# A decoder layer on one core: the second causal mask moves from GpSimd to TensorE

## The chip, the core and the metric

The kernel runs on one core of a Trainium2 chip. A core has five engines that run side by side and meet through semaphores: TensorE (PE, matrix products, with weight loads of its own shown as PEld), VectorE (DVE), ScalarE (ACT), GpSimd (POOL) and SyncE (SP, which issues transfers). Products land in PSUM, eight banks of 128 partitions by 2 KB; all else lies in SBUF. The metric is the time of one execution in microseconds (us).

## The reference, cut to what matters

Sixteen sequences of 128 tokens by 128 features go through one layer: a minimal GRU (three gates and a scan), causal self-attention with 16 heads of 8 features, a gated feed-forward block, cross-attention to a context, and a mixture of eight experts of which two are chosen. The part that the change touches is the softmax of the self-attention:

```python
mask = (kidx <= W + j) & (kidx >= j + 1) & ((kidx >= W) | (cidx > 0))
scores = jnp.where(mask[None, None], scores, jnp.finfo(scores.dtype).min)
attn = jax.nn.softmax(scores, axis=-1)
out = jnp.einsum('bhcqk,bhckd->bhcqd', attn, vv)
```

A sequence is one window of 128, so this is plain causal attention: query q sees keys up to q.

## The kernel before

**Tiles.** Each of the 16 sequences is one tile k of 128 by 128. Every stage is a small function of k, and every engine has a list, written out by hand or by a planner, that says in which order it runs these functions for all tiles: PE 542 entries, ACT 485, DVE 510, POOL 226, SP 74. An engine runs its list strictly in order; an entry waits on semaphores (`after`) for its inputs. Tiles are pipelined: while the last stages of one tile run, the first stages of tiles far ahead are under way. Most buffers have two copies (`b = k % 2`).

**PSUM banks.** `HOME` gives each stage and tile one of the eight banks. `bank_free` makes PE wait until the last user of that bank has been read.

**Start.** SP and ACT issue the loads. PE runs 9 warming products (`keep_busy`, 128 by 512, on data that nobody reads), turns the weights (`w_gru`, `w_qkv`, `w_gate`, `w_ei`, ...) as their transfers land, and starts the GRU of the first tiles (`gru_turn`, `gru_gates`, `gru_turn_back`) and the projections of the context (`ctx_turn`, `ctx_project`). ACT evicts nearly all of that.

**Attention.** Queries and keys are split into three bf16 parts, go through DRAM (`parts_save`, `parts_stack` on SP) and come back stacked over 72 partitions so that one bf16 product has fp32 accuracy. `scores(k, n)` computes four heads with queries on partitions into a bank (four products of L897); one more product, the identity times the constant `above` (L899, 296 columns: only those behind MROWS = 53), adds -1e30 above the diagonal. DVE takes the row maxima (`maxima`), POOL splits them (`max_split`), PE turns them (`max_turn`), ACT copies them, SP puts them into the stacked queries (`max_stack`). `scores_turned(k, n)` then computes the same four heads with keys on partitions, maximum already subtracted (four products of L919, each a group of its own). ACT takes the exponential of the bank (`exponentials`, L1705). That result is not masked yet: two times a tile POOL's `keep_causal` (L523) zeroes the entries of later keys in two of the four banks at once, columns from 53 on. `att_values` waits for both selects (`att_kept`) and multiplies by the values, 32 column-tiled products.

**The rest of a tile.** `att_back`, `att_turn`, `att_project`, the feed-forward block (`ffn_*`, L964 and L987), cross-attention (`xat_*`), experts (`moe_*`, L1046). POOL computes the powers of -0.5 for all norms (`*_power`, L464), residuals, and part of the experts' sum. The last tile ends on DVE with `moe_layernorm(15)`; SP stores the rows.

Of the kernel before, what the change touches and what calls it, by code (L numbers as in the profile page):

```python
# [5 lines left out]
P = 128  # L6
# [8 lines left out]
MROWS = SROWS - QROWS  # L15
# [15 lines left out]
    "w_gru": "0",  # L31
    "gru_turn": "6130635251015364",
    "gru_gates": "6564665631347415",
    "w_qkv": "1",
    "ctx_turn": "0751373176661643",
    "w_ox": "4",
    "gru_turn_back": "7115525220167562",
    "w_gate": "3",
    "qkv_turn": "2043375324264473",
    "w_kq": "4",  # L40
    "qk_project": "2102272754237473",
    "w_ei": "0",
    "w_ej": "2",
    "v_project": "1610750457135003",
    "ctx_project": "7051505346162653",
    "w_m0": "0",
    "w_up": "2",
    "scores": "3127056563626562452440236442443333403164421350137725676407743707",
    "w_out": "4",
    "max_turn": "0245200515644061",  # L50
    "w_m1": "7",
    "probs": "0403141313405274312373664520265241600260432415523754465205655757",
    "att_values": "4410675465665645",
    "att_back": "3474671451562134",
    "att_turn": "5602511353530173",
    "att_project": "5175052773534032",
    "ffn_turn": "2015063551744601",
    "ffn_gate": "5367621631374704",
    "ffn_up": "3115173226106260",
    "ffn_down": "3671500753312560",  # L60
    "xat_turn": "1410670705106321",
    "xat_scores": "4737600607156332",
    "xat_turn_probs": "6712150724311715",
    "xat_values": "3333726551352157",
    "moe_turn": "1726034121131434",
    "moe_logits": "6007031017147427",
    "moe_experts_0": "0774730225456601",
    "moe_experts_1": "4226576422270232",
}
WEIGHTS = ("w_gru", "w_qkv", "w_ox", "w_gate", "w_kq", "w_ei", "w_ej", "w_m0", "w_up", "w_out", "w_m1")  # L70
READER = {
    "w_gru": "w_gru",
    "gru_turn": "gru_xT",
    "gru_gates": "gru_tanh",
    "w_qkv": "w_qkv",
    "ctx_turn": "ctx_T",
    "w_ox": "w_ox",
    "gru_turn_back": "gru_x1",
    "w_gate": "w_gate",
    "qkv_turn": "qkv_xT",  # L80
    "w_kq": "w_kq",
    "qk_project": "qkv_rest",
    "w_ei": "w_ei",
    "w_ej": "w_ej",
    "v_project": "max_v",
    "ctx_project": "ctx_kv",
    "w_m0": "w_m0",
    "w_up": "w_up",
    "scores": "max_max",
    "w_out": "w_out",  # L90
    "max_turn": "max_mT",
    "w_m1": "w_m1",
# [28 lines left out]
att_scores_ps att_p att_kept att_vT_ps att_vT att_o_ps att_rd att_o att_oT_ps att_oT att_y_ps att_x2  # L121
# [12 lines left out]
def decoder_layer(nc, x, ctx, mask, w_mix, Wg, bg, Wv, bv, Wd, bd, w_attn, Wqkv, Wo, w_ffn, Wgate, Wup,  # L134
# [4 lines left out]
    with ExitStack() as stack:  # L139
# [23 lines left out]
        above = sb("above", [P, 4, P], BF16)  # L163
        rows_q = sb("rows_q", [P, P], BF16)
# [108 lines left out]
        def _(sp):  # L273
# [93 lines left out]
            parts_save(3)  # L367
            load_ctx(3)
            max_stack(1)
# [14 lines left out]
            parts_stack(7)  # L384
            parts_save(8)
            max_stack(6)
# [3 lines left out]
            max_stack(8)  # L390
            store(0)
            parts_stack(9)
            parts_save(10)
            max_stack(9)
            parts_stack(10)
            store(1)
            store(2)
# [3 lines left out]
            store(3)  # L401
            max_stack(10)
            parts_stack(12)
            parts_save(13)
            parts_stack(13)
            max_stack(11)
            parts_save(14)
            parts_save(15)
            max_stack(12)
            parts_stack(14)  # L410
            max_stack(13)
            parts_stack(15)
            store(4)
            max_stack(14)
            max_stack(15)
            store(5)
# [13 lines left out]
        def _(pool):  # L430
# [35 lines left out]
            def gru_power(k):  # L466
                b = k % 2
                power(ss[:, 0, b:b + 1], rs[:, 0, b:b + 1], "gru_ss", k, "gru_rs", "gru_xn")

            def qkv_power(k):  # L470
                b = k % 2
                power(ss[:, 1, b:b + 1], rs[:, 1, b:b + 1], "qkv_ss", k, "qkv_rs", "qkv_xn")

            def ffn_power(k):
                b = k % 2
                power(ss[:, 2, b:b + 1], rs[:, 2, b:b + 1], "ffn_ss", k, "ffn_rs", "ffn_xn")

            def ffn_ln_power(k):
                b = k % 2
                power(mv[:, 0, b, 1:2], lrs[:, 0, b:b + 1], "ffn_mv", k, "ffn_rs1", "ffn_y1")  # L480

            def xat_ln_power(k):
                b = k % 2
                power(mv[:, 1, b, 1:2], lrs[:, 1, b:b + 1], "xat_mv", k, "xat_rs", "xat_y2")

            def moe_ln_power(k):
                b = k % 2
                power(mv[:, 2, b, 1:2], lrs[:, 2, b:b + 1], "moe_mv", k, "moe_rs", "moe_out")
# [52 lines left out]
            gru_power(0)  # L541
            gru_power(1)
            gru_power(2)
            gru_decay(0)
            gru_power(3)
            gru_power(4)
            gru_decay(1)
            qkv_power(0)
            causal_tiles()
            gru_decay(2)  # L550
            qkv_power(1)
            qk_low(0)
            gru_power(5)
            gru_decay(3)
            qkv_power(2)
            gru_power(6)
            gru_decay(4)
            qk_low(1)
            qkv_power(3)
            gru_decay(5)  # L560
            qkv_power(4)
            gru_power(7)
            gru_decay(6)
            qk_low(2)
            max_split(0)
            qkv_power(5)
            gru_power(8)
            qk_low(3)
            qkv_power(6)
            keep_causal(0, 0)  # L570
            max_split(1)
            keep_causal(0, 1)
            qk_low(4)
            max_split(2)
            keep_causal(1, 0)
            qk_low(5)
            keep_causal(1, 1)
            ffn_power(0)
            ffn_residual(0)
            gru_decay(7)  # L580
            gru_power(9)
            keep_causal(2, 0)
            max_split(3)
            ffn_power(1)
            keep_causal(2, 1)
            ffn_residual(1)
            qkv_power(7)
            ffn_ln_power(0)
            gru_decay(8)
            qk_low(6)  # L590
            max_split(4)
            xat_residual(0)
            xat_ln_power(0)
            ffn_power(2)
            keep_causal(3, 0)
            ffn_ln_power(1)
            keep_causal(3, 1)
            qk_low(7)
            qkv_power(8)
            moe_add(0)  # L600
            max_split(5)
            xat_residual(1)
            ffn_residual(2)
            keep_causal(4, 0)
            gru_power(10)
            keep_causal(4, 1)
            ffn_ln_power(2)
            xat_ln_power(1)
            gru_power(11)
            keep_causal(5, 0)  # L610
            ffn_power(3)
            max_split(6)
            qk_low(8)
            xat_residual(2)
            moe_add(1)
            keep_causal(5, 1)
            gru_power(12)
            ffn_power(4)
            xat_ln_power(2)
            ffn_residual(3)  # L620
            ffn_ln_power(3)
            max_split(7)
            gru_decay(9)
            xat_residual(3)
            ffn_power(5)
            keep_causal(6, 0)
            moe_add(2)
            ffn_residual(4)
            keep_causal(6, 1)
            ffn_ln_power(4)  # L630
            qkv_power(9)
            max_split(8)
            xat_ln_power(3)
            gru_power(13)
            moe_ln_power(0)
            gru_decay(10)
            xat_residual(4)
            ffn_power(6)
            qk_low(9)
            ffn_residual(5)  # L640
            xat_ln_power(4)
            ffn_ln_power(5)
            keep_causal(7, 0)
            xat_residual(5)
            gru_power(14)
            ffn_residual(6)
            moe_ln_power(1)
            moe_add(3)
            keep_causal(7, 1)
            keep_causal(8, 0)  # L650
            qkv_power(10)
            gru_power(15)
            moe_add(4)
            keep_causal(8, 1)
            ffn_ln_power(6)
            xat_ln_power(5)
            gru_decay(11)
            ffn_power(7)
            ffn_residual(7)
            gru_decay(12)  # L660
            max_split(9)
            qk_low(10)
            ffn_power(8)
            moe_ln_power(2)
            qkv_power(11)
            xat_residual(6)
            moe_add(5)
            ffn_residual(8)
# [2386 lines left out]
```

## Time and profile before

| | |
|---|---|
| median of 3 runs | 230.51 us (229.73 to 230.94) |
| the profiled execution | 230.77 us, of which 229.0 us from the first to the last instruction (the span) |
| busy share of the span | PE 92%, PEld 77%, DVE 81%, ACT 75%, POOL 61% |
| granted TensorE clock, mean | 0.982 of full |

Busy time of an engine is the time in which at least one of its instructions runs. Matmuls overlap in the pipeline and their ends are modelled, so a busy PE need not be at its peak; the start of one product to the start of the next tells more.

### The profile page before, as it was taken

What the parts mean: (1) busy time and instruction counts of PE and PEld (TensorE: products, weight loads), DVE (VectorE), ACT (ScalarE), POOL (GpSimd) and SP (SyncE); (2) the same over time, 40 slices, a digit from 0 to 9 for tenths busy, and PEclk for the clock granted to TensorE, in tenths of its full rate; (3) what the DMA queues carried; (4) which work ended last, traced back from release to release, by engine and by line L of the source; (5) the groups of instructions that cost most, each with busy time, mean ns of one, the idle gap of its engine ahead of it and who ended that gap; (6) DMA issues with size and microseconds to landing.
All of it is one profiled execution on the core that took longest, in us unless ns stands there. A gap on an engine that the chain in (4) does not pass through costs nothing.

```text
span 229.0 us, 6962 instructions
## 1 busy us (share of the span) xinstructions
PE 210.0 (92%) x2169; PEld 175.6 (77%) x2169; DVE 184.5 (81%) x667; ACT 171.8 (75%) x663; POOL 140.0 (61%) x302
## 2 busy tenths in 40 slices
PE   7868989999999999999999999999999999998640
PEld 3657978899987989899788898888778898883210
DVE  2563776639787998988799899999989878999983
ACT  5867977798597898869798979985768868556530
POOL 5442553475655775856857858766665866539542
PEclk9997999999999999999999999999999999999995
DMA  4896363657454323000500254546340000000000
GB/s 102 250 261 181 87 157 106 161 130 152 113 149 100 105 51 105 5 0 21 146 4 1 67 132 134 149 110 148 107 113 9 26 17 3 16 0 13 22 20 27
DMA packets 33715, 20.05 MB, mean 88 GB/s; under 512 B 20496, under 2 KB 31248, under 8 KB 33680
## 3 DMA queue, kind: packets, MB, share of 16 engines
q1 hardware_dynamic: 32992, 19.35, 32.7%
q8 instruction: 18, 0.29, 0.6%
q10 hardware_dynamic: 688, 0.26, 0.4%
q14 instruction: 17, 0.14, 0.2%
HBM read 14.16 MB, written 5.24 MB: 85 GB/s over the span
## 4 chain that ended last, share of the span: by engine, by line
PE 66%; DVE 11%; issue 6%; SPq 5%; POOL 4%; DMA 4%; ACT 3%; POOLq 0%; DVEq 0%; ACTq 0%
PE ps L964 11%; PE ps L1046 7%; PE ps L929 6%; PE ps L842 6%; PE ps L987 6%; PE ps L919 5%; PE ps L897 5%; PE ps L856 4%; SPq L276 3%; PE ps L899 3%; DMA raw<-in_L_ffn_Wi_dram 3%; PE ps L876 2%; PE ps L884 2%; PE ps L953 2%; PE ps L939 1%
## 5 line engine op out<-in xcount | busy, mean ns | idle before, releaser
L2371 DVE TENSOR_REDUCE neg_max<-ps 128x4 f32<-128x512 f32 x64 | 42.7, 677 | 2.9 <-PE ps L899 2.7
L464 POOL TENSOR_TENSOR lrs<-mv,neghalf 128x1 f32<-128x1 f32 x48 | 26.1, 549 | 29.2 <-DVE mv L2416 12.2
L1705 ACT ACTIVATE probs<-ps 128x512 f32<-128x512 f32 x64 | 38.2, 608 | 1.9 <-PE ps L919 1.8
L464 POOL TENSOR_TENSOR rs<-ss,neghalf 128x1 f32<-128x1 f32 x48 | 26.9, 564 | 15.2 <-ACT junk L1623 14.5
L964 PE MATMUL ps<-xT,guT 128*128 128x128 f32 x256 | 33.7, 276 | 0.0
L964 PEld LDWEIGHTS ps<-xT,guT 128*128 128x128 f32 x256 | 31.3, 192 | 1.7 <-issue 1.0
L1046 PE MATMUL ps<-w_moe,y2T 128*128 128x512 f32 x64 | 32.4, 596 | 0.0
L523 POOL TENSOR_SCALAR_AFFINE_SELECT probs<-probs 128x600 f32<-128x600 f32 x32 | 24.2, 757 | 11.0 <-ACT probs L1705 10.5
L897 PE MATMUL ps<-k_stack,q_stack 125*128 125x128 bf16 x256 | 24.9, 219 | 0.1
L919 PE MATMUL ps<-q_stack,k_stack 128*128 128x128 bf16 x256 | 24.8, 219 | 0.1
L919 PEld LDWEIGHTS ps<-q_stack,k_stack 128*128 128x128 bf16 x256 | 18.7, 99 | 4.6 <-issue 3.3
L1628 ACT ACTIVATE xn<-x_all,rs 128x128 f32<-128x128 f32 x48 | 19.6, 410 | 2.0 <-POOL rs L464 1.7
L1784 ACT ACTIVATE terms<-ps,moe_c 128x128 f32<-128x128 f32 x64 | 18.2, 369 | 3.6 <-DVE moe_c L2482 3.3
L897 PEld LDWEIGHTS ps<-k_stack,q_stack 125*128 125x128 bf16 x256 | 17.9, 98 | 3.1 <-issue 1.4
L899 PE MATMUL ps<-above,identb 128*128 128x296 bf16 x64 | 18.7, 292 | 0.0
L1623 ACT ACTIVATE junk<-x_all 128x129 f32<-128x129 f32 x48 | 15.4, 321 | 4.3 <-DVE x_all L2389 2.6
L929 PE MATMUL ps<-probs,values 128*32 128x128 f32 x512 | 17.3, 275 | 0.3 <-ACT terms L1784 0.3
L987 PE MATMUL ps<-outT,hidden 128*128 128x128 f32 x128 | 17.3, 278 | 0.1
L987 PEld LDWEIGHTS ps<-outT,hidden 128*128 128x128 f32 x128 | 15.6, 192 | 0.8 <-DVE hidden L2400 0.5
L929 PEld LDWEIGHTS ps<-probs,values 128*32 128x32 f32 x512 | 13.1, 109 | 2.6 <-issue 1.1
L2343 DVE TENSOR_SCALAR y<-z,mv,lrs 128x128 f32<-128x128 f32 x32 | 13.2, 416 | 2.3 <-POOL lrs L464 2.0
L535 POOL TENSOR_TENSOR term_pairs<-terms 128x256 f32<-128x256 f32 x16 | 11.6, 726 | 5.2 <-ACT terms L1784 5.0
(156 smaller groups left out, 587.1 us busy)
## 6 DMA issues: line engine op xcount, KB each, us to landing
q_stack<-qk_scratch SPq DMA_DIRECT2D x48, 96.0 KB
k_stack<-qk_scratch SPq DMA_DIRECT2D x48, 96.0 KB
qk_scratch<-qk_parts SPq DMA_DIRECT2D x16, 192.0 KB, 2.2
ctx_sb<-in_ctx_dram SPq DMA_DIRECT2D x4, 256.0 KB, 3.2
qk_scratch<-qk_parts SPq DMA_DIRECT2D x16, 64.0 KB, 2.5
out_dram<-x_all SPq DMA_DIRECT2D x16, 64.0 KB, 1.6
x_all<-in_x_dram SPq DMA_DIRECT2D x2, 256.0 KB, 3.0
raw<-in_L_ffn_Wi_dram SPq DMA_DIRECT2D x1, 512.0 KB, 6.1
```

Of the source, the lines that this page charges most:

```text
L464: nc.gpsimd.tensor_tensor(dst, src, neghalf[:], ALU.pow).then_inc(S[rsd], 1)
L523: nc.gpsimd.affine_select(out=later, in_=later, compare_op=ALU.is_ge, fill=0.0, base=MROWS, pattern=[[0, 2 * QUARTER], [1, P - MROWS]], ch ...
L897: nc.tensor.matmul(home[:, h, :], q_stack[0:SROWS, r, QUARTER * n + h, :], k_stack[0:SROWS, r, QUARTER * n + h, :], start=(h == 0), stop=F ...
L899: nc.tensor.matmul(home[:, :, MROWS + 1:P], identb[:], above[:, :, MROWS + 1:P], start=False, stop=True).then_inc(S["max_scores_ps"], 1)
L919: last = nc.tensor.matmul(home[:, j, :], k_stack[:, r, h, :], q_stack[:, r, h, :], start=True, stop=True)
L929: last = nc.tensor.matmul(view("att_values", k)[COLS * j:COLS * j + COLS, r, :], values[:, b, t, QUARTER * r + j, :], probs[:, b, 2 * r + ...
L964: last = nc.tensor.matmul(view(fill, k)[:, n, :], guT[:, g, n * P:(n + 1) * P], xT[:, 1, b, :], start=True, stop=True)
L987: last = nc.tensor.matmul(view("ffn_down", k)[:, 0, :], hidden[:, b, n, :], outT[:, n, :], start=(n == 0), stop=(n == FF - 1))
L1046: nc.tensor.matmul(as_one(view(fill, k)), y2T[:, b, :], w_moe[:, 4 * n:4 * n + 4, :], start=True, stop=True).then_inc(S[("moe_m0_ps", "moe ...
L1628: nc.scalar.activation(xn[:, n, b, :], src, ACT.Copy, scale=rs[:, n, b:b + 1]).then_inc(S[done], 1)
L1705: nc.scalar.activation(probs[:, b, n, :, :], view("probs", 4 * k + n), ACT.Exp, scale=HD ** -0.5).then_inc(S["att_p"], 1)
L2371: nc.vector.tensor_reduce(neg_max[:, b, QUARTER * n:QUARTER * n + QUARTER], view("scores", 4 * k + n), AX_X, ALU.max, negate=True).then_in ...
```

## The change

The select on POOL is gone. A second constant, `below`, holds -1e30 where the key lies behind the query; `scores_turned` ends with the identity times `below`, 300 columns, in the same accumulation group, and the exponential turns those entries into zeros. `att_values` waits for the exponentials alone. The orders of all engines, the banks, and the order in which weights are turned are laid out anew (the lists differ in many places, mostly by a few entries). Three warming products are added near the start, and waits that other waits imply are left out (`power`'s second one, one in `moe_weights`); `moe_experts` gets one, on `moe_xT`.

```diff
@@ gpsimd
                 nc.gpsimd.affine_select(out=above[:], in_=zeros, compare_op=ALU.is_ge, fill=MASKED, base=0,
                                         pattern=[[0, 4], [-1, P]], channel_multiplier=1).then_inc(S["causal"], 1)
+                nc.gpsimd.affine_select(out=below[:], in_=zeros, compare_op=ALU.is_ge, fill=MASKED, base=0,
+                                        pattern=[[0, 4], [1, P]], channel_multiplier=-1).then_inc(S["causal"], 1)
-            def power(src, dst, ready, k, rsd, used):
-                after_all(pool, (ready, k + 1), (used, k - 1))
+            def power(src, dst, ready, k, rsd):
+                after(pool, ready, k + 1)
-            def keep_causal(k, g):
-                b = k % 2
-                after(pool, "att_p", 4 * k + 2 * g + 2)
-                later = probs[:, b, 2 * g:2 * g + 2, :, MROWS:P].rearrange("p n j q -> p (n j) q")
-                nc.gpsimd.affine_select(out=later, in_=later, compare_op=ALU.is_ge, fill=0.0, base=MROWS,
-                                        pattern=[[0, 2 * QUARTER], [1, P - MROWS]], channel_multiplier=-1).then_inc(S["att_kept"], 1)
             row_patterns()
             gru_power(0)
+            causal_tiles()
             gru_power(1)
...
-            qkv_power(0)
-            causal_tiles()
...
@@ tensor
+                if k == 0 and n == 0:
+                    pe.wait_ge(S["causal"], 2)
...
-                    last = nc.tensor.matmul(home[:, j, :], k_stack[:, r, h, :], q_stack[:, r, h, :], start=True, stop=True)
-                last.then_inc(S["att_scores_ps"], 1)
+                    nc.tensor.matmul(home[:, j, :], k_stack[:, r, h, :], q_stack[:, r, h, :], start=(j == 0), stop=False)
+                nc.tensor.matmul(home[:, :, MROWS:P], identb[:], below[:, :, MROWS:P], start=False, stop=True).then_inc(S["att_scores_ps"], 1)
             def att_values(k):
-                after(pe, "att_kept", 2 * (k + 1))
+                after(pe, "att_p", 4 * (k + 1))
...
+                after(pe, "moe_xT", k + 1)
                 bank_free(pe, fill, k)
...
@@ sync
+            max_stack(1)
             load_ctx(3)
-            max_stack(1)
...
+            max_stack(6)
             parts_save(8)
-            max_stack(6)
...
@@ vector
-                after(dve, "moe_z", k - 1)
+            half_biases()
             w_gru()
-            half_biases()
-            rows_k_in(0)
+            w_qkv()
             gru_input(0)
```

The first entries of PE's list, before and after (9 warming products stand ahead of both):

```
before: w_gru, gru_turn(0), gru_turn(1), gru_gates(0), w_qkv, gru_gates(1), ctx_turn(0), keep_busy(1), w_ox,
        gru_turn(2), gru_turn_back(0), keep_busy(1), gru_turn(3), ctx_turn(1), gru_gates(2), w_gate, qkv_turn(0),
        gru_turn_back(1), w_kq, gru_turn(4), qk_project(0), w_ei, gru_gates(3), gru_turn_back(2), ctx_turn(2), w_ej, ...
after:  w_gru, w_qkv, gru_turn(0), keep_busy(1), gru_turn(1), gru_gates(0), gru_gates(1), ctx_turn(0), w_kq,
        keep_busy(2), gru_turn_back(0), w_ox, gru_turn(2), keep_busy(1), gru_turn(3), ctx_turn(1), keep_busy(1),
        qkv_turn(0), ctx_project(0), gru_turn_back(1), qk_project(0), gru_gates(2), v_project(0), ctx_turn(2),
        gru_gates(3), ctx_project(1), gru_turn(4), w_ei, ...
```

Just ahead of `scores(0, 0)` stand `ctx_project(3)` and `gru_gates(6)` before, `gru_gates(6)` and `ctx_project(4)` after.

## Rows read from the trace of the kernel before

**Rows 1.** The page: busy us by engine; granted clock in 40 slices.

```profile
PE 210.0 (92%) x2169; PEld 175.6 (77%) x2169; DVE 184.5 (81%) x667; ACT 171.8 (75%) x663; POOL 140.0 (61%) x302
...
PEclk9997999999999999999999999999999999999995
```

**Rows 2.** By stretch: length; busy us of PE, PEld, DVE, ACT, POOL; clock; DMA.

```profile
0.00:40.00 40.00, 33.70 (x245) 27.44 (x245) 22.44 (x59) 30.62 (x124) 18.83 (x46) 0.96 0.61 163
40.00:188.90 148.90, 148.27 (x1742) 128.55 (x1740) 128.94 (x449) 121.14 (x456) 100.22 (x218) 1.00 0.34 87
188.90:229.00 40.10, 28.05 (x186) 19.61 (x185) 33.12 (x161) 20.00 (x84) 20.99 (x40) 0.94 0.05 14
```

**Rows 3.** PE in order of time, 60 to 66 us (start, us, line, operation, count).

```profile
60.26 1.06 PE L964 MATMUL ps<-xT,guT 128*128 128x128 f32 x8
61.16 0.39 PE L1016 MATMUL ps<-ctx_kv,y1T 128*128 128x128 f32 x2
...
62.97 0.39 PE L897 MATMUL ps<-k_stack,q_stack 125*128 125x128 bf16 x4
63.19 0.29 PE L899 MATMUL ps<-above,identb 128*128 128x296 bf16 x1
63.32 0.43 PE L1027 MATMUL ps<-ctx_kv,xat_pT 128*128 128x128 f32 x2
...
63.81 0.39 PE L919 MATMUL ps<-q_stack,k_stack 128*128 128x128 bf16 x4
64.03 1.11 PE L987 MATMUL ps<-outT,hidden 128*128 128x128 f32 x8
```

**Rows 4.** The same view, 168 to 170 us.

```profile
168.79 1.02 PE L1046 MATMUL ps<-w_moe,y2T 128*128 128x512 f32 x2
169.65 0.27 PE L842 MATMUL ps<-ident,att_o 128*128 128x128 f32 x1
```

**Rows 5.** Groups by line, shapes apart (busy us, mean ns, idle before and its releaser).

```profile
L1046 PE MATMUL ps<-w_moe,y2T 128*128 128x512 f32 x64 | 32.4, 596 | 0.0
...
L897 PE MATMUL ps<-k_stack,q_stack 125*128 125x128 bf16 x256 | 24.9, 219 | 0.1
L919 PE MATMUL ps<-q_stack,k_stack 128*128 128x128 bf16 x256 | 24.8, 219 | 0.1
L523 POOL TENSOR_SCALAR_AFFINE_SELECT probs<-probs 128x600 f32<-128x600 f32 x32 | 24.2, 757 | 11.0 <-ACT probs L1705 10.5
...
L919 PEld LDWEIGHTS ps<-q_stack,k_stack 128*128 128x128 bf16 x256 | 18.7, 99 | 4.6 <-issue 3.3 <-DMA q_stack<-nmT 0.5
L899 PE MATMUL ps<-above,identb 128*128 128x296 bf16 x64 | 18.7, 292 | 0.0
...
L929 PE MATMUL ps<-probs,values 128*32 128x128 f32 x512 | 17.3, 275 | 0.3 <-ACT terms L1784 0.3
...
L929 PEld LDWEIGHTS ps<-probs,values 128*32 128x32 f32 x512 | 13.1, 109 | 2.6 <-issue 1.1 <-POOL probs L523 0.6
```

**Rows 6.** PE's groups from 0 to 40 us, then from 188.9: first and last.

```profile
L856 PE MATMUL ps<-xT,gruT 128*128 128x128 f32 x42 | 6.4, 293 | 0.7 <-DVE gruT L2293 0.5 <-DVE x_all L2359 0.2
...
L907 PE MATMUL ps<-identb,nm_parts 128*128 128x128 bf16 x1 | 0.2, 216 | 0.3 <-issue 0.3
...
L1046 PE MATMUL ps<-w_moe,y2T 128*128 128x512 f32 x24 | 11.9, 597 | 0.0
...
L939 PE MATMUL ps<-ident,att_vT 128*128 128x128 f32 x2 | 0.4, 272 | 0.0
```

**Rows 7.** PE in order of time, 13 to 16 us.

```profile
13.03 0.68 PE L876 MATMUL ps<-qkv_xT,qkvT 128*128 128x128 f32 x4
15.34 0.66 PE L773 MATMUL ps<-ident,raw 128*128 128x128 f32 x4 [1.63 <-DMA raw<-in_L_ffn_Wi_dram]
```

**Rows 8.** Busy time of ACT alone from 3.7 to 26.1 us.

```profile
3.70:26.10 22.40, 17.80 (x78) 0.92 0.70 189
```

**Rows 9.** POOL in order of time at 11.5 us: the select that makes `above`.

```profile
11.48 0.74 POOL L458 TENSOR_SCALAR_AFFINE_SELECT above<-flat 128x512 bf16<-128x512 bf16 x1
```

More of the change, by code:

```diff
@@ L30 @@
 HOME = {
-    "w_gru": "0",
-    "gru_turn": "6130635251015364",
-    "gru_gates": "6564665631347415",
+    "w_gru": "6",
     "w_qkv": "1",
-    "ctx_turn": "0751373176661643",
-    "w_ox": "4",
-    "gru_turn_back": "7115525220167562",
-    "w_gate": "3",
[L39 to L47, printed above, removed]
@@ L60 @@
[L60 to L68, printed above, removed]
+    "gru_turn": "2664301274424434",
+    "gru_gates": "2164356143660120",
+    "ctx_turn": "7706314043525747",
+    "w_kq": "0",
+    "gru_turn_back": "6500355430304677",
@@ new lines @@
+    "w_ox": "4",
+    "qkv_turn": "5142623626267673",
+    "ctx_project": "2274530746647035",
+    "qk_project": "1601324607214654",
+    "v_project": "5210713033625034",
+    "w_ei": "7",
+    "w_m0": "2",
+    "w_gate": "3",
+    "w_ej": "6",
+    "w_up": "7",
+    "scores": "4731520335122516562113453062567321115746305754066710121503311326",
+    "w_out": "5",
+    "w_m1": "6",
+    "max_turn": "5750214266347027",
+    "probs": "7426735322142040242274170566215070450073134124634716645011171065",
@@ L778, in keep_busy @@
                 for _ in range(count):
[L779 removed]
+                    nc.tensor.matmul(as_one(banks[3][:]), warm[:, 0:P], warm[:], start=True, stop=True)
             pe.wait_ge(S["const_dve"], 1)
@@ new lines, in _ @@
+            qkv_turn(0)
+            ctx_project(0)
+            gru_turn_back(1)
+            qk_project(0)
+            gru_gates(2)
+            v_project(0)
+            ctx_turn(2)
+            gru_gates(3)
+            ctx_project(1)
+            gru_turn(4)
+            w_ei()
+            qkv_turn(1)
+            gru_turn(5)
+            qk_project(1)
+            w_m0()
+            gru_gates(4)
+            ctx_turn(3)
+            gru_turn_back(2)
+            gru_turn(6)
+            ctx_project(2)
@@ L1198, in _ @@
             scores(5, 1)
+            ffn_down(1)
+            moe_turn(0)
+            scores_turned(3, 3)
+            scores(5, 2)
             v_project(5)
             qkv_turn(7)
-            scores_turned(3, 3)
-            moe_turn(0)
-            scores(5, 2)
+            moe_logits(0)
+            scores(5, 3)
+            moe_experts(0, 0)
             qk_project(7)
-            moe_logits(0)
+            ffn_turn(2)
+            att_values(3)
             scores_turned(4, 0)
-            ffn_turn(2)
@@ L1232, in _ @@
             att_values(4)
+            scores(6, 3)
+            qk_project(8)
+            moe_turn(1)
             scores_turned(5, 1)
-            scores(6, 2)
-            moe_turn(1)
             att_back(4)
+            moe_experts(1, 1)
             xat_turn(2)
-            att_project(3)
+            ffn_turn(3)
+            scores_turned(5, 2)
+            max_turn(6)
+            scores(7, 0)
+            xat_scores(2)
+            att_turn(4)
             moe_logits(1)
-            scores(6, 3)
+            scores_turned(5, 3)
@@ L1424, in _ @@
-            scores(11, 2)
-            moe_logits(7)
-            scores_turned(10, 3)
-            scores(11, 3)
-            qk_project(14)
-            moe_experts(7, 0)
+            scores(11, 1)
+            scores_turned(10, 0)
+            scores(11, 2)
+            scores_turned(10, 1)
+            scores(11, 3)
+            scores_turned(10, 2)
+            moe_turn(7)
+            v_project(12)
+            scores_turned(10, 3)
+            qkv_turn(14)
+            moe_experts(7, 0)
@@ new lines, in _ @@
+            moe_logits(7)
+            att_values(10)
+            max_turn(11)
+            gru_turn_back(15)
+            ffn_turn(9)
+            scores(12, 0)
+            qk_project(14)
+            att_back(10)
+            scores(12, 1)
+            ffn_gate(9)
+            scores(12, 2)
+            ffn_up(9)
+            moe_turn(8)
+            att_turn(10)
+            scores_turned(11, 0)
+            scores(12, 3)
+            moe_experts(7, 1)
+            att_project(10)
+            ffn_down(9)
@@ L1834, in _ @@
+            gru_copy(6)
+            w_gate()
             qkv_copy(2)
-            qkv_squares(3)
-            gru_normalize(6)
-            w_m0()
-            ctx_copy(3)
-            ctx_copy(4)
-            gru_copy(6)
-            gru_tanh(5)
-            qk_high(2)
+            w_ej()
+            gru_tanh(5)
+            v_copy(1)
+            ctx_copy(4)
+            qk_high(2)
+            gru_squares(8)
+            ctx_copy_kv(3)
+            ctx_copy_kv(4)
+            qkv_squares(3)
```

1764 lines of the change are left out of this document (842 added, 922 removed).

## The prediction

> **What bounds the kernel now.** I read the shares of busy time first, then three long stretches, then the groups by line, and last single matmuls in order of time, because a busy TensorE (PE) is not yet a full one. PE shows 92% busy and its clock is full but for a dip early and the end [rows 1]. By stretches it is busy 33.7 of the first 40 us, 148.3 of the next 148.9 us, and 28.1 of the last 40.1 us, in which VectorE (DVE) is busy 33.1 us [rows 2].
>
> Busy PE time can hide bubbles, since ends overlap. So I take start to start. Eight fp32 matmuls of L964 begin at 60.26 and the next group at 61.16: 0.112 us each. Four bf16 products of L919 take 63.81 to 64.03: 0.055 each. One mask product of L899 takes 63.19 to 63.32: 0.13 [rows 3]. Two fp32 products of 512 columns take 168.79 to 169.65, 0.43 each [rows 4]. The groups give the counts: 64 of 512 columns (27.5 us), 512 bf16 of L897 and L919 (28.2), 64 masks (8.4), 16 att_values of 32 products (17.3 by their busy time) [rows 5], and of the page's 2169 products 1017 others [rows 1]: 11 warming ones at 0.43 (4.7) and 1006 that I put at 0.112 (112.7). That is some 198 us of streaming in 229.0: 31 us of holes. The same sum for the 245 products before 40 us (18 groups) is 28 us, so 12 us of holes; for the 186 after 188.9 (13 groups) 26 us, so 14 of holes; what is left for the middle is 5 to 6 us in 149 [rows 2, 6]. So in the middle PE is full in truth, the start waits on data and copies, and the end is the last tiles' chain through DVE.
>
> By the Trainium skill (Perfetto Trace Analysis, Identifying the Most-Contended Engine) matmul busy time is a bad measure of the distance to the limit, and weight-load busy time a good one. The row for that is 175.6 us, 77% [rows 1]; read so, PE would have 53 us free and the new products would cost nothing. The starts say otherwise, and I go by them; what the rule would give is the second rival.
>
> **The change part by part.** *The masks.* Removed are 32 selects on GpSimd (POOL), 0.757 us each, 24.2 us in all [rows 5]. POOL is 61% busy and does not set the end. What is worth something is the wait they put between the exponentials and att_values: att_values' weight loads waited 0.6 us on POOL in the whole run [rows 5]; PE had other work in front. So the removal gives 0.6 us, at most a little over 1 with the waits behind it.
>
> Added are 64 products, identb times `below[:, :, 53:128]`, four heads of 75 columns: 300 columns, bf16. The trace has the twin: L899, 296 columns, 0.13 us from its start to the next. A bank of scores with its mask takes 62.97 to 63.32, 0.35; a bank of scores_turned without one 63.81 to 64.03, 0.22; again 0.13 [rows 3]. Its weight load runs under the stream before it. From above, L899's mean duration of 0.292 us (18.7 us for 64) [rows 5] would bound it, if nothing overlapped; from below nothing, if it fell in holes. The middle has 5 to 6 us of holes and 60 of the 64 products go there, so I take 0.133 (300/296 of 0.131): 64 x 0.133 = **+8.5 us**, all ahead of att_values(15), on the engine that sets the pace. Ends: 0 and 18.7. By the Trainium skill (TensorE: Matmul & The Clock Gate, Back-to-back issue gap) a warm product alone costs columns over 2.4 GHz and 2.5 ns, 127.5 ns for 300 columns; 64 of them would be 8.2 us by that page, beside 8.5 by the rows.
>
> *The start.* The old order runs qk_project(0) at 13.03 and then w_ei, whose weights have not landed: the next product starts at 15.34 [rows 7], 1.8 us lost, and the clock falls to its lower level (0.7 in the slice from 17.2 us [rows 1]), which I put at 1.7 us more of PE time. The new order has w_ei seven entries later, behind two gru_gates, a ctx_project and more (2.2 us), w_gate later too, and three more warming products (0.43 each at the lower clock), which lie in holes. But this is not 3.5 us won. ScalarE (ACT) feeds that stretch: 17.8 us busy in the 22.4 us from 3.7 to 26.1 [rows 8], so its holes, 4.6 us, are the most that a better order can win ahead of the first scores; and, by the groups' mean durations, the new list has about 1 us more of ACT work in front of ctx_copy(4), which ctx_project(4) and then scores(0, 0) wait for. On POOL causal_tiles() now stands between gru_power(0) and gru_power(1) and issues two selects of 0.74 us [rows 9]: gru_power(1), then gru_normalize(1) and the second gate product come up to 1.5 us later; a warming product and w_qkv fill that on PE, and I count 0.5 us of delay for the first gru_tanh. DVE has half_biases ahead of w_gru, and waits for three bias columns there: nothing, as w_gru's product ends about when they land. Net, ends 0 and 4.6: I take **-2.0 us**, between the middle and the low end because of the two delays. Behind the first scores a fixed chain (maxima, split, turn, copy, DMA, scores_turned) has the same 4.1 us of PE work (by the spacings above) under it in both orders; nothing is won there.
>
> *The middle.* The lists hold the same entries, a few places apart: some 167 us of work by the spacings above stands ahead of att_values(15) in both, within 3 us at each earlier att_values. With 8.5 us more on PE, ACT, DVE and POOL have that much more time to be ready, and the selects are gone. Of the 5 to 6 us of holes I take back **-1.5 us** (ends: -4 and, if new banks collide, +2).
>
> *Queues.* On SP max_stack(1) passes load_ctx(3), max_stack(6) passes parts_save(8), the stores move: one issue each of about half a microsecond, and the saves behind them now wait for the maxima of an earlier tile. SP has stores and saves waiting for tens of microseconds, so nothing; if a tile's parts came late PE would wait for the landing, up to 2 us once. *Waits left out* (power, moe_weights) were met long before: nothing. The added wait of moe_experts on moe_xT stands behind moe_turn's copy that moe_logits already waits for: nothing.
>
> *The tail.* From att_values(15) on both PE lists have 60 entries, all but a few the same ones, and DVE has 34 us of work (by the groups' mean durations) behind att_out(15) in both. The 40.1 us there stay, give or take 2.
>
> Sum: 8.5 - 2.0 - 1.5 = +5.0 us. The profiled execution took 230.77 us (span 229.0 and 1.8 around it): 235.8. It lies 0.26 above the median of 230.51, so I say **235.5 us**, 2.2% slower.
>
> **The rivals.** *The holes close (same).* Start and middle together give back 7.5 to 9.6 us: ACT runs without a gap (4.6) and the middle loses 3 to 5 of its holes. For it: nearly every named stall of the start is moved. Against it: the delay of gru_power(1), and the holes of the middle are many small ones. Time 229.4 to 231.7.
>
> *PE is not full (faster).* If quartets of bf16 products are bound by their weight loads (L919's last 0.099 us each against 0.055 between starts [rows 3, 5]), a product of 300 columns would give the loader time to run ahead. The place is every scores_turned in the middle, the price of a mask falls from 0.133 towards 0, and what start and middle gain stays: 230.5 - 3.5 = 227.0. It decides once the net price is under 0.04 us (2.4 us in all, less than the gains by 1.1). Against it: the products of both quartets start 0.055 apart, so the loads run ahead already. (This is what the rule on weight loads of the Trainium skill, Perfetto Trace Analysis, would have here; the starts of this trace speak against it.)
>
> *The mask costs its duration (dearer).* At 0.292 us each, were the bank held until its end: 18.7 - 3.5 = +15.2, 245.7. Against it: L899's own neighbour starts after 0.13.
>
> **How the numbers follow.** Forecast case 0.63: mask 8.3 to 9, start 0 to -4.6, middle -3 to +2, tail 2 either way: 232 to 239.5. Holes close: 0.12. PE not full: 0.17. Dearer: 0.08. Half a per cent (1.15 us) is about what a measurement of this kernel can tell from no change. So faster 0.17, same 0.12, slower 0.71. The range, 228.0 to 239.5, takes in the closing of the holes and the upper half of the faster case, and leaves out 0.17.
>
> **What would show it.** In the changed profile: 64 new products, each about 0.13 us from its start to the next; PE full from some 40 us on; att_values(15) at about 194 instead of 188.9, with 40 us behind it; no gap of 1.8 us at 13 us and no dip of the clock there; POOL near 116 us busy. I am wrong if att_values(15) starts before 190, if PE's holes ahead of it come to under 9 us, or if what follows it is shorter than 38 us.

## The result and the profile after

The changed kernel takes **234.36 us** (median of 4 runs, 233.34 to 236.05), the kernel before 230.12 (4 runs, 229.68 to 230.94, same chip): ratio 1.0179, 95% interval 1.0106 to 1.0252. The prediction said 235.5 us, 228.0 to 239.5, slower with a chance of 0.71. The profiled execution took 235.31 us with a span of 233.3, so its own rows lie 0.95 us above the median; the one of before lay 0.65 above this median (0.26 above the one known to the prediction).

The page after, against [rows 1]: 67 products more (64 masks, 3 warming), POOL down to 117.8 us, no dip of the clock at 17 us, but one in the third slice from the end (215.8 to 221.6 us).

```profile
PE 217.2 (93%) x2236; PEld 180.8 (78%) x2236; DVE 183.0 (78%) x667; ACT 172.7 (74%) x663; POOL 117.8 (50%) x271
...
PEclk9999999999999999999999999999999999999795
```

Stretches after, with the columns of [rows 2], and the third beginning at att_values(15) again:

```profile
0.00:40.00 40.00, 36.19 (x303) 28.99 (x304) 22.75 (x61) 33.06 (x135) 19.46 (x50) 1.00 0.65 171
40.00:192.40 152.40, 151.07 (x1754) 131.28 (x1752) 127.18 (x448) 119.94 (x446) 77.22 (x182) 1.00 0.33 83
192.40:233.30 40.90, 29.97 (x186) 20.57 (x185) 33.07 (x160) 19.71 (x83) 21.14 (x40) 0.89 0.04 12
```

The last stretch holds 186 products, as before, so all 67 new ones lie ahead of att_values(15). That entry comes at 192.38 us (188.94 before [rows 2]): **+3.4 us**. The tail behind it is 40.9 us (40.1): **+0.8**. In the first 40 us PE now gets through 303 products instead of 245.

PE in order of time, after: the place of [rows 7], att_values(0), the place of [rows 3], att_values(15):

```profile
13.22 0.67 PE L840 MATMUL ps<-qkv_xT,qkvT 128*128 128x128 f32 x4
13.73 0.83 PE L820 MATMUL ps<-xT,gruT 128*128 128x128 f32 x6
...
38.10 0.54 PE L895 MATMUL ps<-probs,values 128*32 128x128 f32 x12
...
63.33 0.39 PE L885 MATMUL ps<-q_stack,k_stack 128*128 128x128 bf16 x4
63.56 0.29 PE L886 MATMUL ps<-below,identb 128*128 128x300 bf16 x1
63.69 0.39 PE L861 MATMUL ps<-k_stack,q_stack 125*128 125x128 bf16 x4
...
192.38 0.53 PE L895 MATMUL ps<-probs,values 128*32 128x128 f32 x12
```

The gap of 1.8 us behind qk_project(0) is gone, and the new product L886 takes 63.56 to 63.69: 0.13 us from its start to the next, though its duration reads 0.29. Sixty-four of them are 8.3 us of streaming, yet att_values(15) comes only 3.4 us later. The sum of the prediction, made product by product (each start to the next, less the spacing of its kind), has the rest: holes of PE ahead of att_values(15) fell from 18.2 us to 12.8, from 11.0 to 7.0 in the first 40 us and from 7.2 to 5.8 behind them. The levels hang on the spacings taken, by 2 to 3 us in all; the falls move by under 1 us.

Medians below are of all executions of a kernel; ratios leave out the slow ones, over 1.5% above its fastest (some of the kernel before, old_kernel_late_wei, new_order_no_mask, no_mask_old_sp, new_order_old_sp and new_order_stack_first), and where the profiled execution was such a one only its waits are read.

### The profile page after: what moved, and what is told of

Read it like the earlier page. It is cut to its first block, busy times and chain, and to the rows that moved or that the text cites. A ratio compares the mean times of both kernels' runs of the same rounds, so it can differ in the third digit from the quotient of the medians.

```text
span 233.3 us, 6998 instructions
## 1 busy us (share of the span) xinstructions
PE 217.2 (93%) x2236; PEld 180.8 (78%) x2236; DVE 183.0 (78%) x667; ACT 172.7 (74%) x663; POOL 117.8 (50%) x271
## 4 chain that ended last, share of the span: by engine, by line
PE 68%; DVE 10%; ACT 7%; DMA 5%; issue 4%; POOL 3%; SPq 2%; POOLq 0%; DVEq 0%; ACTq 0%
PE ps L930 11%; PE ps L1013 6%; PE ps L806 6%; PE ps L861 5%; PE ps L953 5%; PE ps L885 5%; PE ps L895 5%; PE ps L820 3%; DMA k_stack<-qk_scratch 3%; PE ps L863 3%; PE ps L886 3%; PE ps L840 2%; PE ps L968 2%; PE ps L743 2%; DVE acc L2455 2%
## 5 line engine op out<-in xcount | busy, mean ns | idle before, releaser
L2340 DVE TENSOR_REDUCE neg_max<-ps 128x4 f32<-128x512 f32 x64 | 43.5, 683 | 5.4 <-PE ps L863 4.9
L467 POOL TENSOR_TENSOR lrs<-mv,neghalf 128x1 f32<-128x1 f32 x48 | 26.1, 549 | 37.9 <-DVE mv L2420 14.8
L1013 PE MATMUL ps<-w_moe,y2T 128*128 128x512 f32 x64 | 34.2, 626 | 0.0
L861 PEld LDWEIGHTS ps<-k_stack,q_stack 125*128 125x128 bf16 x256 | 18.4, 97 | 4.2 <-DMA k_stack<-qk_scratch 1.4
L1753 ACT ACTIVATE terms<-ps,moe_c 128x128 f32<-128x128 f32 x64 | 18.2, 369 | 4.0 <-PE ps L1013 2.2
L886 PE MATMUL ps<-below,identb 128*128 128x300 bf16 x64 | 18.7, 292 | 0.0
L526 POOL TENSOR_TENSOR qk_parts<-qk_rest,qk_parts 128x256 bf16<-128x256 f32 x16 | 10.7, 671 | 11.6 <-ACT qk_parts L1651 11.5
```

What stands on the lines that cost most here:

```text
L861: nc.tensor.matmul(home[:, h, :], q_stack[0:SROWS, r, QUARTER * n + h, :], k_stack[0:SROWS, r, QUARTER * n + h, :], start=(h == 0), stop=F ...
L886: nc.tensor.matmul(home[:, :, MROWS:P], identb[:], below[:, :, MROWS:P], start=False, stop=True).then_inc(S["att_scores_ps"], 1)
L1013: nc.tensor.matmul(as_one(view(fill, k)), y2T[:, b, :], w_moe[:, 4 * n:4 * n + 4, :], start=True, stop=True).then_inc(S[("moe_m0_ps", "moe ...
L2340: nc.vector.tensor_reduce(neg_max[:, b, QUARTER * n:QUARTER * n + QUARTER], view("scores", 4 * k + n), AX_X, ALU.max, negate=True).then_in ...
```

## The experiments

Ratios are against runs of the kernel before on the same chip (medians 230.93, 230.54 and 230.85 on three chips; ratios to the changed kernel are quotients of these). Where a ratio is missing, one execution alone was left to count. "Values" is the start of att_values in the profiled execution, "tail" what lies behind the last one.

| kernel | median, us | ratio (95% interval) | values(0) | values(15) | tail |
|---|---|---|---|---|---|
| before | 230.12 | 1 | 42.49 | 188.94 | 40.1 |
| after | 234.36 | 1.0179 (1.0106 to 1.0252) | 38.10 | 192.38 | 40.9 |
| new_order_two_masks | 242.00 | 1.0474 (1.0416 to 1.0533) | 38.84 | 198.19 | 41.9 |
| new_order_no_mask | 232.07 | 1.0042 (0.9994 to 1.0090) | | | |
| old_order_pe_mask | 235.53 | 1.0208 (1.0140 to 1.0275) | 41.70 | 193.35 | 42.1 |
| new_order_pool_mask | 236.68 | 1.0256 (1.0189 to 1.0324) | 38.55 | 194.49 | 39.5 |
| old_kernel_late_wei | 230.48 | 0.9973 (0.9938 to 1.0009) | 39.73 | 186.89 | 42.0 |
| new_order_old_sp | 246.12 | none | 38.89 | 200.85 | 39.6 |
| no_mask_old_sp | 245.43 | 1.0550 (1.0447 to 1.0654) | | | |
| new_order_one_swap | 237.49 | 1.0319 (1.0243 to 1.0394) | 39.38 | 194.87 | 40.9 |
| new_order_stack_first | 238.16 | 1.0269 (1.0169 to 1.0368) | | | |
| new_order_tail_clock | 234.42 | 1.0172 (1.0125 to 1.0219) | 38.17 | 192.34 | 39.6 |
| old_kernel_wei_clock | 229.69 | 0.9967 (0.9931 to 1.0003) | 39.83 | 185.83 | 41.4 |
| old_kernel_no_above | 226.98 | 0.9856 (0.9803 to 0.9910) | 39.69 | 184.81 | 40.1 |

### What a mask product costs: two of them, and none

```diff
@@ scores_turned, new_order_two_masks
+                nc.tensor.matmul(home[:, :, MROWS:P], identb[:], below[:, :, MROWS:P], start=False, stop=False)
                 nc.tensor.matmul(home[:, :, MROWS:P], identb[:], below[:, :, MROWS:P], start=False, stop=True)
@@ scores_turned, new_order_no_mask: each product a group of its own, as before
-                nc.tensor.matmul(home[:, :, MROWS:P], identb[:], below[:, :, MROWS:P], start=False, stop=True)
```

new_order_two_masks:

> The changed kernel with each product with below issued twice (the output does not change by it: the mask is added twice). Full-queue theory: 64 x 0.13 = 8.4 us more, 242 to 243.5 us. Rival (room beside the weight loads): 234 to 236 us. Dearer by its whole duration of 0.29 us: 253 us.

new_order_no_mask:

> The changed kernel without the 64 products with below; it leaves out the second causal mask (for keys from row 53 on the attention is not causal). Full-queue theory: 8.4 us below the changed kernel's 234.4, so 225.5 to 227 us, that is 3 to 4 us below the kernel before, which is what the new orders are worth. Rival (the orders lose, the mask is free): 233 to 235 us.

Two masks: 242.0 us, 7.6 more than one (6.8 by the ratios), 0.11 to 0.12 for each of the 64, as a full PE would have it. PE in order of time shows the pair; the stretch behind it (columns of [rows 2]) runs from 38 us to att_values(15) and has PE busy for 160.05 of 160.20 us:

```profile
62.94 0.29 PE L886 MATMUL ps<-below,identb 128*128 128x300 bf16 x1
63.07 0.29 PE L887 MATMUL ps<-below,identb 128*128 128x300 bf16 x1
63.20 0.22 PE L871 MATMUL ps<-identb,nm_parts 128*128 128x128 bf16 x1
```

```profile
38.00:198.20 160.20, 160.05 (x1860) 139.00 (x1858) 128.71 (x449) 123.36 (x457) 77.66 (x183) 1.00 0.32 80
```

No mask: 232.07 us, only 2.3 less than one (3.2 by the ratios), where 7 to 9 were expected of a full PE. So the first 64 products cost 0.04 to 0.05 us each and the second 64 cost 0.11 to 0.12. What PE waits for without them is in the waits of its profile (engine, line, releaser: us in all, times, longest), here followed by the one such wait of the changed kernel:

```profile
PE ps L861 <- DMA k_stack<-qk_scratch: 3.0, 5, 1.4
...
PE ps L885 <- DMA q_stack<-nmT: 0.9, 1, 0.9
```

```profile
PE ps L861 <- DMA k_stack<-qk_scratch: 0.8, 1, 0.8
```

The first products of scores wait for queries and keys on their way through DRAM, and those of scores_turned once for the maxima. That these waits are the limit a little under the present load of PE is likely, not shown: the profiled execution took 237.02 us, 5 above its median, and the waits come to 3.9 us.

### The orders alone, the masks alone

old_order_pe_mask is the kernel before (all its lists, banks and waits) with the selects out and the products in; new_order_pool_mask is the changed kernel with the products out and the selects back.

```diff
@@ old_order_pe_mask, gpsimd: all 32 like this, and scores_turned as in the change
-            keep_causal(0, 0)
@@ new_order_pool_mask, gpsimd: all 32, each where its second exponential had ended
+            keep_causal(0, 0)
```

old_order_pe_mask:

> The mask alone: orders, banks and waits of the kernel before, but the 64 products with below end scores_turned and the 32 selects on POOL are gone. Full-queue theory (a mask product takes 0.13 us of a PE that has no room): 64 x 0.13 = 8.4 us, less at most 1 us for the waits on POOL: 237 to 238.5 us, all of it ahead of att_values(15). Rival (PE is not full, the products fall beside weight loads, and the loss of the change is one of its orders): 229 to 231 us.

new_order_pool_mask:

> The new orders, banks and waits with the mask of the kernel before: no products with below, the 32 selects back on POOL, each put into POOL's list where the second of its two exponentials ended in the changed kernel's trace. Full-queue theory: the selects cost little, since PE has other work queued while POOL works: 226 to 228.5 us, faster than both kernels. Rival (what the change wins comes from taking the select's wait out, not from the orders): 229 to 231 us. Rival (the orders lose): 233 us or more.

In the old lists the swap costs 4.8 us (1.0208): of 8.3 us of products 4.4 reach att_values(15), because the holes close there too (in the middle 7.2 to 4.6) and att_values(0) comes 0.8 earlier, with a clock that stayed full at the start; from att_values(0) to att_values(15) it is 5.2 us more. In its profiled execution, the longest of four (237.31 us), the tail is 2 us longer, at a mean clock of 0.85 against 0.94. The new lists then bring 1.0208 to 1.0179, 0.7 us, which their intervals don't separate. They do start earlier, 41.70 to 38.10 at att_values(0), 3.6 us; at att_values(15) 1.0 of it is left (193.35 to 192.38). Part of that lead is work put off: 14 products (eight of scores with two masks, four of L840) that the old list runs ahead of att_values(0) stand behind it in the new one, 1.2 us by their spacings. In the new lists the selects are not cheaper than the products (236.68): att_values waited for POOL's selects 1.7 us in four places, scores 2.6 us for k_stack. That is where the rival that the orders lose was put (233 us or more). My places for the selects are not tuned, so this says only that lists and mask belong together.

### The start alone

```diff
@@ old_kernel_late_wei, tensor (and on vector behind gru_out(2))
             qk_project(0)
-            w_ei()
             gru_gates(3)
             gru_turn_back(2)
             ctx_turn(2)
+            w_ei()
```

> The kernel before, selects on GpSimd, with only w_ei moved (behind ctx_turn(2) on TensorE, behind gru_out(2) on VectorE), so that the 1.8 us gap at 13 us and the dip of the clock behind it should go; att_values(0), at 42.49 us before, should come 2 to 4 us earlier. Theory A (what the start gains is given back in the middle, because there other waits than TensorE set the pace of the kernel with selects): att_values(15) comes at most 1 us earlier, time 229.5 to 231. Theory B (my step of the start, a gain that stays): att_values(15) at 185.5 to 187.5, time 227 to 229.

The gap at the start shrinks to 0.4 us and the dip is gone, att_values(0) comes 2.8 us earlier, att_values(15) 2.05 earlier, and the time is the same. My theory A was wrong in its place: the middle gave little back, the tail did, in the profiled execution. PE in the tail, of the kernel before and of this one:

```profile
213.15 2.74 PE L1046 MATMUL ps<-w_moe,y2T 128*128 128x512 f32 x6
218.66 0.33 PE L842 MATMUL ps<-ident,y 128*128 128x128 f32 x1 [2.77 <-DVE y L2343]
...
219.59 1.96 PE L1046 MATMUL ps<-w_moe,y2T 128*128 128x512 f32 x4
```

```profile
211.11 2.74 PE L1046 MATMUL ps<-w_moe,y2T 128*128 128x512 f32 x6
216.62 0.33 PE L842 MATMUL ps<-ident,y 128*128 128x128 f32 x1 [2.76 <-DVE y L2343]
...
217.75 3.76 PE L1046 MATMUL ps<-w_moe,y2T 128*128 128x512 f32 x4
```

The same gap of 2.8 us stands ahead of the last tile's experts; here the granted clock fell behind it (0.74 from 216 to 218 us, 0.50 from 218), and the last four products took 3.76 us instead of 1.96. The last tile's sum of the experts stands behind them.

### SP's list

```diff
@@ new_order_one_swap, sync
-            max_stack(6)
             parts_save(8)
+            max_stack(6)
@@ new_order_stack_first, sync
-            max_stack(12)
             parts_stack(14)
+            max_stack(12)
```

new_order_old_sp has all of SP's old list in the changed kernel, no_mask_old_sp the same without the products.

new_order_old_sp:

> The changed kernel with SP's list of the kernel before. Theory A (maxima, stores and saves in a new order on SP make a tile's parts land late, seen as 0.8 us of TensorE waiting for k_stack at 159 us): the waits on the DMA of k_stack and q_stack go, time 232.5 to 233.5. Theory B (my step: the new SP order costs nothing, TensorE is full): 234 to 235.

no_mask_old_sp:

> The changed kernel without the 64 below products (the attention is then not causal for the keys from row 53 on) and with SP's list of the kernel before. Without the products and with the new SP list the time was 232.07, with waits for k_stack in the middle. Theory A (the SP order sets the floor that the kernel meets without the products): 227 to 229.5. Theory B (the floor is elsewhere, in the transfers and the engines that fill them): 231 to 233.

new_order_one_swap:

> The changed kernel with a single pair of SP entries put back: parts_save(8) ahead of max_stack(6). Theory A (the SP list is what the new orders stand on: max_stack(6) then waits behind a save whose parts ScalarE and GpSimd finish near 83 us, and scores_turned of tile 6 waits for k_stack's partner nmT): a wait of 1.5 to 1.9 us on the DMA of q_stack<-nmT near 84 us, and, as TensorE is full behind it, most of it in the end: 235.2 to 236.5. Theory B (my step: one issue of half a microsecond, queues cost nothing): 234 to 234.8 and no such wait.

new_order_stack_first:

> The changed kernel with a single pair of SP entries exchanged: parts_stack(14) ahead of max_stack(12), which waited 2.2 us for ScalarE at 150.6 us with the parts saved behind it. Theory A (that entry is why scores of tile 14 waited 0.8 us for k_stack at 159.2 us): the wait goes, att_values(15) at 191.3 to 191.9, 233.3 to 234. Theory B (something else on TensorE takes its place, or max_stack(12) is now late itself): att_values(15) not before 192.2, 234.2 to 235.5.

The first two refuted both of their theories: the old list does not save 1 us, it costs some 8 or more (242.32 to 247.80 us). The single pair shows why. SP in order of time, after, then with the pair exchanged:

```profile
80.33 0.72 SPq L352 DMA_DIRECT2D q_stack<-nmT  x1
82.42 0.39 SPq L326 DMA_DIRECT2D qk_scratch<-qk_parts  x1
```

```profile
83.44 0.39 SPq L326 DMA_DIRECT2D qk_scratch<-qk_parts  x1
83.88 0.54 SPq L328 DMA_DIRECT2D qk_scratch<-qk_parts  x1
84.52 0.73 SPq L352 DMA_DIRECT2D q_stack<-nmT  x1
...
84.70 0.39 PE L993 MATMUL ps<-ctx_kv,xat_pT 128*128 128x128 f32 x2
86.72 0.40 PE L885 MATMUL ps<-q_stack,k_stack 128*128 128x128 bf16 x4 [1.63 <-DMA q_stack<-nmT]
```

In the new orders of ACT and POOL the parts of tile 8 are ready later than the maxima of tile 6. With the save in front, max_stack(6) is issued at 84.52 instead of 80.33, and scores_turned of tile 6, which comes at 83.9 in the changed kernel without waiting, now waits 1.63 us. att_values(15) comes 2.5 us later, of which 1.3 were there at att_values(0) already (see the last section), so 1.2 for one pair; the median moved by 3.1, and whether the rest belongs to the pair as well is not shown. With the whole list PE waits 5.1 us for q_stack and 4.3 for k_stack:

```profile
PE ps L885 <- DMA q_stack<-nmT: 5.1, 4, 1.9
PE ps L861 <- DMA k_stack<-qk_scratch: 4.3, 3, 1.9
```

new_order_stack_first aimed at the one wait left in the changed kernel and missed it: the entry that waits for ScalarE at 150.6 us is max_stack(11), ahead of parts_stack(13), not the pair that I exchanged. What it shows is its theory B: max_stack(12), now behind six issues, is late itself (waits of PE, columns as above).

```profile
PE ps L885 <- DMA q_stack<-nmT: 1.7, 1, 1.7
```

### The tail's clock

```diff
@@ new_order_tail_clock, tensor: also behind moe_turn(13) and moe_turn(14); bank 5, free by then
             xat_scores(15)
+            keep_clock(1)
             moe_turn(13)
@@ old_kernel_wei_clock, tensor (old_kernel_late_wei with it)
             moe_experts(14, 1)
+            keep_clock(5)
             moe_turn(15)
```

new_order_tail_clock:

> The changed kernel with three more warming products of 512 columns (0.43 us each) in a free bank in the tail's holes, behind xat_scores(15), moe_turn(13) and moe_turn(14). Theory A (the fall of the granted clock from 217.2 to 220.6 us is what the tail lost, 40.9 us against 40.1, and the scatter of the runs): the clock stays full to some 225 us, tail 39.5 to 40.2, time 233.3 to 234, the runs within 1 us. Theory B (DVE sets the tail, the clock there costs nothing): the tail stays within 0.3 us or grows by the products, 234.3 to 235.5.

old_kernel_wei_clock:

> The kernel before (selects on GpSimd) with w_ei later and with five warming products of 512 columns between moe_experts(14, 1) and moe_turn(15), where TensorE stood idle for 2.8 us and the granted clock then fell to half for the last four products of 512 columns (3.76 us instead of some 1.9). Theory A (w_ei later brings 2 us to att_values(15), and the tail's clock took them back): clock full to the last product, tail 39.8 to 40.3 behind att_values(15) at 186.9, time 228 to 229. Theory B (the tail is VectorE's chain, the clock is no cause): 230 to 231.

Neither moved its median by more than the intervals. The tails (columns of [rows 2]) of new_order_tail_clock, old_kernel_late_wei and old_kernel_wei_clock:

```profile
192.30:231.90 39.60, 28.99 (x189) 20.01 (x188) 33.10 (x160) 19.75 (x83) 21.18 (x40) 0.95 0.04 13
```

```profile
186.90:228.90 42.00, 30.00 (x186) 20.31 (x185) 33.18 (x161) 20.06 (x84) 20.98 (x40) 0.86 0.05 14
```

```profile
185.80:227.20 41.40, 30.50 (x190) 20.38 (x190) 33.12 (x161) 20.05 (x84) 21.00 (x40) 0.92 0.05 14
```

In the first, the profiled execution kept its clock (0.95 over the tail, 0.89 without) and its tail is 39.6 us instead of 40.9, yet the four runs are at 233.72 to 235.18. In the second the clock fell all the same, at 217 us, and the tail is 41.4. So a full clock in the tail goes with 39.5 to 40.1 us and a fallen one with 40.9 to 42.1, in the profiles read here. At a full clock the new lists' tail is 39.5 to 39.6 us and the old ones' 40.1. But these products do not reliably keep the clock, and a gain in time is not shown.

### Fewer products in the old lists

```diff
@@ old_kernel_no_above: old_kernel_wei_clock, scores without the above mask
-                nc.tensor.matmul(home[:, :, MROWS + 1:P], identb[:], above[:, :, MROWS + 1:P], start=False, stop=True).then_inc(S["max_scores_ps"], 1)
+                last.then_inc(S["max_scores_ps"], 1)
```

> old_kernel_wei_clock without the 64 products of the above mask: the maxima run over all keys, the softmax takes the same value, since any number not below the row's maximum may be subtracted. 64 x 0.131 = 8.4 us of TensorE less. Theory A (a full queue in both directions): 220.5 to 222.5. Theory B (as in the changed kernel without its below products, most of a product's price is given back as waits for parts and copies, some 0.04 us each stays): 225.5 to 228.

226.98 us, as theory B had it, 2.7 less than with the mask: 0.042 us a product of 0.131 in the streams [rows 3], a third, as in the changed kernel. This is the version that beats both: 3.1% under the changed kernel, 1.4% under the one before. In the profiles att_values(15) moved by 1.0 only; the rest is the tail, whose clock stayed full here (0.95) with the same five warming products that had failed next door.

## Why the prediction was right, and which steps were not

**PE is full where it is busy: right, upwards.** A second set of 64 products cost 6.8 to 7.6 us. That settles two rivals. Products at 0.292 us each (dearer) are out: 0.13 from start to start. PE not full is out too, and with it what the rule on weight loads of the Trainium skill (Perfetto Trace Analysis, Identifying the Most-Contended Engine) would have made of 78% weight-load time: 22% of room in which a second mask should have been free. The gap of a product alone in the Trainium skill (TensorE: Matmul & The Clock Gate, Back-to-back issue gap) gave 127.5 ns for 300 columns; the trace agrees, at 0.13 us.

**The mask, +8.5 us: the streaming right (8.3), the effect too large.** Taken as added in full, with 1.5 us given back by the middle. By old_order_pe_mask 5.2 us show between att_values(0) and att_values(15) in unchanged lists, and the swap costs 4.8 us in all; in the new lists the products cost 2.3 to 3.2. They fall partly into holes that the trace showed and that I counted, 5 to 6 us of the middle, and I let them absorb too little.

**The start, -2.0 us: right at its own mark, wrong behind it.** scores(0, 0) came 2.3 us earlier (28.21 to 25.88). But the step "behind the first scores a fixed chain ... nothing is won there" failed: scores_turned(0, 0) came 3.75 us earlier. The chain is not fixed: the four quarters of scores(0) stand in PE's list with other entries between them, and behind the turn the old list has eight products of L828 (36.66 to 37.62 us) right ahead of scores_turned; the new one runs them ahead of the turn. Before, then after; first and fourth quarter, the turn of the maxima, the first scores_turned:

```profile
28.21 0.39 PE L897 MATMUL ps<-k_stack,q_stack 125*128 125x128 bf16 x4
...
31.01 0.39 PE L897 MATMUL ps<-k_stack,q_stack 125*128 125x128 bf16 x4
...
33.87 0.22 PE L907 MATMUL ps<-identb,nm_parts 128*128 128x128 bf16 x1 [0.27 <-issue]
...
37.62 0.39 PE L919 MATMUL ps<-q_stack,k_stack 128*128 128x128 bf16 x4
```

```profile
25.88 0.38 PE L861 MATMUL ps<-k_stack,q_stack 125*128 125x128 bf16 x4
...
27.96 0.39 PE L861 MATMUL ps<-k_stack,q_stack 125*128 125x128 bf16 x4
...
30.88 0.22 PE L871 MATMUL ps<-identb,nm_parts 128*128 128x128 bf16 x1 [0.21 <-issue]
...
33.87 0.39 PE L885 MATMUL ps<-q_stack,k_stack 128*128 128x128 bf16 x4
```

First to fourth quarter 2.80 us before, 2.08 after; from the turn to scores_turned 3.75 and 2.99. Holes to 40 us fell by 4.0, twice the term.

**The middle, -1.5 us: right in size (7.2 to 5.8), not in its reason.** I gave the credit partly to POOL's selects and to the lists. More work on PE closes holes by itself: in old_order_pe_mask with the selects gone as well, and in new_order_two_masks, where only products were added and PE is idle for 0.15 us of the stretch to att_values(15), against 1.3 in the changed kernel (152.40 less 151.07). Of the 2.6 us that the start's lead over old_order_pe_mask loses, 1.2 are the 14 products put off, and behind 159.2 us scores wait 0.8 us for k_stack. The rest, 0.6, stays open.

**Queues, nothing: wrong.** "SP has stores and saves waiting for tens of microseconds, so nothing" had it upside down. Just because SP's entries wait, whatever stands behind one waits too: an exchanged pair costs 1.2 us in the trace, the old list 8 or more. That the term still came out near nothing fits a list of SP that was changed together with ACT's and POOL's; the new SP list under the old ones of the others was not run.

**The tail, 0: +0.8,** within its 2 us. It goes with the granted clock, which fell to 0.50 from 217.2 to 220.6 us; in new_order_tail_clock, with a full clock, the same tail is 39.6. The profiled execution is of the longer two: 235.31 and 236.05 us went with a mean granted clock of 0.98, 233.34 and 233.41 with 0.99. In new_order_tail_clock the same two clocks do not part the times (235.18 and 233.95, 233.72 and 234.90), so how much of the scatter is the clock's stays open.

Together: +8.8 of products (the three warming ones among them), -4.0 at the start, -1.4 in the middle, +0.8 in the tail is +4.2, beside +4.3 in the span (229.0 to 233.3); the forecast had +5.0. The holes close, the rival at 229.4 to 231.7, came half true: they gave back 5.4 us where it asked for 7.5. In this sum of one execution the start was mis-sized by 2.0 and the tail by 0.8 the other way.

By the kernels the near hit is in part luck. The forecast without its masks was 227.0 us, 3.5 under the kernel before; new_order_no_mask took 232.07, 1.0 above by the ratios, not clear of no change. So the lists brought nothing that can be measured, and the masks cost 2.3 to 3.2 us in them, not 8.5. By the other way round, masks first, they cost 4.8 and the lists gave back 0.7. Either way the forecast had the masks some 4 to 6 us too dear and the lists 3 to 4.5 too good, and the two errors cancelled. Right is the mechanism at PE, products of 0.13 us on an engine with little room; what the room is worth to the lists was not.

## What to carry to other kernels

A product added to an engine that is full costs its spacing from start to start, not its duration; one taken away gives back only what the next limit leaves, here a third. The price rises with the load, so one measured by adding does not hold for taking away. A list of a strict queue, SP's above all, is part of the change: for each entry that is moved, compare when it and its neighbour become ready, since the later one holds the earlier up. Read the tail with the clock beside it, because a gain ahead of it can vanish there.

## What the hardware showed that I had not expected

The same transfer can land at different times. Two kernels with the same lists up to there issue the save of tile 0 within 0.01 us of each other (17.64 and 17.63); the entry behind it starts at 19.92 in the changed kernel and at 21.48 in new_order_one_swap, and scores(0, 0) comes at 25.88 and 27.15, after PE lists that ran alike to 0.02 us:

```profile
17.64 0.55 SPq L328 DMA_DIRECT2D qk_scratch<-qk_parts  x1
...
19.92 0.37 SPq L344 DMA_DIRECT2D q_stack<-qk_scratch  x1
```

```profile
17.63 0.55 SPq L328 DMA_DIRECT2D qk_scratch<-qk_parts  x1
...
21.48 0.38 SPq L344 DMA_DIRECT2D q_stack<-qk_scratch  x1
...
27.15 0.38 PE L861 MATMUL ps<-k_stack,q_stack 125*128 125x128 bf16 x4 [1.30 <-DMA k_stack<-qk_scratch]
```

The second part of that save, 64 KB, landed after 2.2 us in the one and 3.8 in the other. That is 1.3 us between executions of nearly one kernel, half of the spread of the changed kernel's runs. It is one trace of each, perhaps of two chips; the cause is not shown.

The clock does not follow a gap each time. The gap of 1.63 us for w_ei's weights stands in the kernel before and in old_order_pe_mask alike; the clock fell behind it in the first (0.7 in the slice from 17.2 us) and stayed full in the second. The gap of 2.8 us in the tail left it full in the kernel before and was followed by half of it in old_kernel_late_wei.
